# Cross-attention scores as three fp32r passes instead of one fp32 matmul, with a new order of work

## The chip, the cores and the metric

The kernel runs on one core of a Trainium2 chip. The metric is the device time of one execution in microseconds (us); TensorE (PE) multiplies matrices, and its weight loads (PEld) are a queue of their own in the profile; VectorE (DVE), ScalarE (ACT) and GpSimd (POOL) work on rows of 128 partitions; SyncE (SP) issues DMAs. TensorE writes only to PSUM, of which this kernel uses eight banks of 512 fp32 columns.

## The reference

One decoder layer on 32 batches of 112 tokens with 256 features, with a context of 375 rows per batch:

```python
x = x + attn(layernorm(x), W_qkv, W_out)                 # 16 heads of 16, window of 64, causal
x = x + xattn(layernorm(x), ctx, Wq, Wkv, Wo, rel_bias)  # 16 heads of 16
x = x + ffn(layernorm(x), router, gate, up, down)        # 8 experts, top 2

# xattn:
q = (h @ Wq).reshape(B, S, H, D).transpose(0, 2, 1, 3)
k, v = split((ctx @ Wkv).reshape(B, K, 2, H, D))
scores = einsum('bhsd,bhkd->bhsk', q, k) + bias
out = einsum('bhsk,bhkd->bshd', softmax(scores), v) @ Wo
```

The change touches `scores` of `xattn` alone: for each batch 16 heads, each 112x16 times 16x375.

## The kernel before

The program has two stages. Stage one runs both attentions and the router for the 32 batches and scatters the rows to expert buffers. Stage two (from L1050 on) runs 64 blocks of 128 rows through the experts.

Stage one is a software pipeline written out by hand. `PERIOD` lists the steps of one period, each with the batch it works on: `S0@1` in period i works on batch i+1. `plan` unrolls the list, and every engine runs those steps of the list that are its own, in this order. Nothing else sets the order: engines meet only at semaphores, so an `@` tells the order within an engine and not the time at which two engines run a step. A period is one batch of every step.

TensorE's steps, with the line that its matmuls carry: `xT`, `x2T`, `x3T`, `on`, `onC` (two transposes, L512); `qk` (L526); `v`, `wo`, `woc`, `rt` (L518); `S4`, the self scores (L535); `sT0` to `sT3` (four transposes, L544); `pvS` (L553); `ot`, `otc` (L560); `q2`, the cross queries (L568); `k0`, `k1`, the cross keys (L575); `v0`, `v1`, the context values (L583); `S0` to `S3`, the cross scores of four heads each (L594); `p0` to `p15` (three transposes of a head's scores, L603); `pv0` to `pv3` (L616); `pf` (L624, L625). In one period of before they stand in this order:

```
pv1 S0@1 p8 x3T@-1 p10 qk@3 sT0@2 p14 rt@-1 S1@1 sT3@2 sT1@2 k0@2 p15 pvS@2 p12 pv2 p13 p3@1 ot@2 pv3 p1@1 p0@1
on@2 pf@-1 S2@1 p7@1 wo@2 p2@1 k1@2 v0@2 otc p4@1 S3@1 onC p6@1 p5@1 x2T@2 woc v1@2 S4@3 pv0@1 q2@2 p11@1 v@3
xT@4 p9@1 sT2@3
```

PSUM banks: the four banks `S0` to `S3` are filled together by one group, `S0`..`S3` or `S4`, and hold one head (or four self heads) each. They are single: the next group waits until DVE has drained all four. Banks P and Q take turns for `sT` and `p`. Banks A and B take turns for all other TensorE steps (`BANK_AB`), so a bank must be drained two such steps later.

`cross_scores` (L588 to L596) makes one matmul for each of the four row tiles of 32 partitions: the stationary side is `q2`, 32x112 (the queries times a 0/-1 mask of half a row tile, two masks, made by ACT in `halves`, step `q2m`), the moving side is `k2`, 32x376, copied from the bank by ACT in steps `k0c`, `k1c`. Both are fp32. The trace shows an fp32 matmul as two LDWEIGHTS and two MATMUL rows.

`keys` and `context_values` already work in another way: context and weights are split into a high part, rounded to fp32r, and a low part, the remainder rounded to fp32r, and `PASSES` lists the three products that are added up: high by high, low by high, high by low. Each product is one LDWEIGHTS and one MATMUL row.

Behind the scores: DVE adds the bias and takes the minimum (steps `t0` to `t15`, L847), POOL subtracts (`u`, L466), TensorE transposes (`p`), ACT takes the exponential (`e`, L729), TensorE multiplies with the values (`pv`). DVE's other steps are `sm` (self scores, L835), the statistics `ln1` to `ln3`, the normalisations `nrm`, `nrmc` (L823, L824), the sums `x1` (L925) and `x2` (L947), `cl` (low part of the context, L936) and the router (`lg`, `rcA`, `rcB`, and `pfD` with L878 to L886).

Of the kernel before, what the change touches and what calls it, by code (L numbers as in the profile page):

```python
# [25 lines left out]
P = 128  # L26
# [37 lines left out]


PERIOD = """
t9@-1 e7@-1 pv1 xn@2 x1 su2@2 xn2 su0@2 v0c e2@-1 ln2 t11@-1 u10 e4@-1 t10@-1 nrmc@-2 oncc@-2 t12@-1 t15@-1
t14@-1 t13@-1 S0@1 x2Tc p8 su3@2 Lc@1 x2@-2 v1c ln3@-2 u1@1 e5@-1 ch@1 x3T@-1 e6@-1 oc0@-1 su1@2 q2m sm2@1
e11@-1 p10 sm0@1 sm3@1 qk@3 vc@1 e9@-1 xTc@2 sT0@2 p14 x3@-2 rt@-1 sm1@1 S1@1 t1 sT3@2 t3 sT1@2 k0@2 sE2@1 p15
pvS@2 p12 oc1@-1 e8@-1 t0 x3Tc@-2 pv2 t2 u0@1 e10@-1 p13 sE0@1 u3@1 p3@1 e14@-1 qkc@2 sE3@1 re@-2 cl@1 sE1@1  # L70
lg@-2 ot@2 pv3 p1@1 sc@-2 p0@1 e15@-1 on@2 pf@-1 S2@1 rcA@-2 p7@1 wo@2 p2@1 k1@2 ln1@3 u4@1 v0@2 otc u7@1
rs1@4 km@3 p4@1 u2@1 S3@1 u6@1 u5@1 onC u8@1 p6@1 k0c@1 t4 t7 p5@1 oTc@1 x2T@2 Lx@3 rs2@2 e12@-1 woc t5 u11@1
v1@2 u9@1 oc2@-1 S4@3 t6 pv0@1 nrm@1 u15@1 q2@2 e13@-1 e3 oc3@-1 p11@1 u14@1 e1 u13@1 rcB@-2 onc@1 st@-3 v@3
e0 xT@4 k1c@1 rs3 p9@1 pfD@-2 u12@1 sT2@3 t8
"""


# [33 lines left out]
def decoder_layer(nc, a, out):  # L111
# [21 lines left out]
    with ExitStack() as outer:  # L133
# [46 lines left out]
        with ExitStack() as st:  # L180
            def s1(name, shape, dt=F32):
                return sb(name, shape, dt, st)
# [46 lines left out]
            x1 = [sa([S, D]) for i in range(NX)]  # L229
            xn2 = sa([S, D])  # L230
            x2T = sa([P, DC, S])
            q2 = [sa([P, DC, 2, S]) for i in range(2)]

            cT = [s1(f"cT_{part}", [P, DC, TPAD], F32R) for part in ("high", "low")]
            wkv = [s1(f"wkv_{part}", [P, DC, 2 * D], F32R) for part in ("high", "low")]
            PASSES = ((0, 0), (1, 0), (0, 1))
            k2 = [sa([P, DC, T + 1]) for i in range(2)]
            v2 = [sa([TP, TC, H, HP]) for i in range(2)]
            z = [sa([S, TPAD]) for i in range(NZ)]
            mC = s1("mC", [S, H])  # L240
# [72 lines left out]
            s_sc = [sem("rows_scattered0"), sem("rows_scattered1")]  # L313
            s_padi = sem("padding_rows_known")

            NCONST, NLATE = 10, 9

            steps = [(w, b) for w, b in plan(B)]
            place = fills(steps)
            taken = {w: n for n, w in enumerate(w for w in steps if w[0][0] == "t" or w[0][:2] == "sm")}  # L320
            su_count = {w: n for n, w in enumerate(w for w in steps if w[0][:2] == "su")}
            u_count = {w: n for n, w in enumerate(w for w in steps if w[0][0] == "u")}

            had = {}
# [23 lines left out]
            def drain_sem(step, b):  # L348
                return drained[place[step, b][0]]
# [6 lines left out]
            def v3(t, n, w, m=P):  # L356

                return t[0:m, 0:n * w].rearrange("p (n w) -> p n w", n=n)

            with nc.Block() as block:  # L360
# [141 lines left out]
                def _(pe):  # L502
# [85 lines left out]
                    def cross_scores(g, b, F_):  # L588
                        if g == 0:
                            drained_wait(pe, "q2", b)  # L590
                        drained_wait(pe, f"k{g // 2}", b)
                        c, k = g // 2, g % 2
                        for r in range(HG):
                            m = pe.matmul(bank[f"S{r}"][0:S, 0:T + 1], q2[b % 2][32 * r:32 * r + 32, c, k, :],  # L594
                                          k2[b % 2][32 * r:32 * r + 32, c, :], start=True, stop=True)
                        m.then_inc(F_, 1)  # L596

                    def probs_back(n, b, B_, F_):
# [100 lines left out]
                def _(act):  # L699
# [14 lines left out]
                    def halves(b):  # L714
                        B_ = filled_wait(act, "q2", b)
                        if b >= 2:
                            filled_wait(act, "S3", b - 2)
                        for p in range(2):
                            m = act.activation(q2[b % 2][:, :, p, :], v3(B_, DC, S), ACT.Copy, scale=hmask[:, p:p + 1])
                        m.then_inc(drain_sem("q2", b), 1)  # L720

                    def cross_probs(n, b):
                        B_ = filled_wait(act, f"p{n}", b)
# [7 lines left out]
                    for step, b in steps:  # L731
# [5 lines left out]
                        elif step == "xTc":  # L737
                            drain("xT", b, xT[:, :, :], lambda t: v3(t, DC, S))
                        elif step == "qkc":
                            drain("qk", b, qk[:, :, :], lambda t: v3(t, 4, S))  # L740
                        elif step == "vc":
                            if b == 0:
                                need(act, s_pool, 1)
                            drain("v", b, vS[:, :, 0:DH], lambda t: v3(t, H, DH, S))
                        elif step[:2] == "sE":
                            r = int(step[2])
                            B_ = filled_wait(act, f"sT{r}", b)
                            if b:
                                filled_wait(act, "pvS", b - 1)
                            act.activation(pTF[r][:, :, :], v3(B_, HG, S, S), ACT.Exp, scale=SCALE)\  # L750
                               .then_inc(drain_sem(f"sT{r}", b), 1)
                        elif step == "oTc":
                            drain("pvS", b, oTF[:, :, :], lambda t: v3(t, NG, S))
                        elif step == "onc":
                            drain("on", b, onT[:, :, :], lambda t: v3(t, DC, S))
                        elif step == "xn2":
                            if b:
                                filled_wait(act, "x2T", b - 1)
                            normalised(1, b, x1[b % NX][:, :], [xn2[:, :]]).then_inc(s_xn2, 1)
                        elif step == "x2Tc":  # L760
                            drain("x2T", b, x2T[:, :, :], lambda t: v3(t, DC, S))
                        elif step == "q2m":
                            halves(b)
                        elif step == "ch":
                            need(act, s_c[b % 2], 16 * (b // 2 + 1))
                            if b:
                                for w in ("k0", "k1", "v0", "v1"):
                                    filled_wait(act, w, b - 1)
                            copy(cT[0][:, :, :], cin[b % 2][:, :, :], s_ch)
                        elif step in ("k0c", "k1c"):  # L770
                            if b >= 2:
                                filled_wait(act, "S3", b - 2)
                            drain(step[:2], b, k2[b % 2][:, int(step[1]), :], lambda t: t[:, 0:T + 1])
                        elif step in ("v0c", "v1c"):
                            if b >= 2:
                                filled_wait(act, "pv3", b - 2)
                            elif b == 0:
                                need(act, s_pool, 2)
                            if step == "v0c":
                                drain("v0", b, v2[b % 2][:, 0:2, :, 0:DH],  # L780
                                      lambda t: t[0:TP, 0:2 * D].rearrange("p (t h d) -> p t h d", t=2, h=H))
                            else:
                                drain("v1", b, v2[b % 2][:, 2, :, 0:DH], lambda t: v3(t, H, DH, TP))
                        elif step[:2] == "oc":
                            g = int(step[2])
                            if g == 0 and b:
                                filled_wait(act, "otc", b - 1)
                            drain(f"pv{g}", b, oTC[:, g, :], lambda t: t[:, 0:S])
                        elif step == "oncc":
                            drain("onC", b, otT[:, :, :], lambda t: v3(t, DC, S))  # L790
                        elif step == "x3":
                            if b >= 2:
                                need(act, s_sc[b % 2], 32 * (b // 2))
                            normalised(2, b, x2[b % 2][:, :], [x3[b % 2][k][:, 0:D] for k in (1, 0)]).then_inc(s_x3, 1)
                        elif step == "x3Tc":
                            drain("x3T", b, x3T[:, :, :], lambda t: v3(t, DC, S))
                        elif step == "re":
                            need(act, s_lg, b + 1)
                            B_ = filled_wait(act, "rt", b)
                            act.activation(ex[:, :], B_[0:S, 0:E], ACT.Exp, bias=nmx[:, :],  # L800
                                           accum_out=zs[:, :]).then_inc(drain_sem("rt", b), 1)
                        elif step[0] == "e":
                            cross_probs(int(step[1:]), b)

                @block.vector
                def _(dve):
# [102 lines left out]
                    for step, b in steps:  # L909
# [22 lines left out]
                        elif step == "cl":  # L932
                            if b == 0:
                                split_weights()
                            need(dve, s_ch, b + 1)
                            dve.tensor_tensor(cT[1][:, :, :], cin[b % 2][:, :, :], cT[0][:, :, :].bitcast(F32),  # L936
                                              ALU.subtract).then_inc(s_cl, 1)
                        elif step == "nrmc":
                            if b:
                                filled_wait(dve, "onC", b - 1)  # L940
# [344 lines left out]
```

## Time and profile before

| | us |
|---|---|
| median of the runs | 1370.25 (1369.9 to 1375.36) |
| profiled execution, its own time | 1372.08 |
| its span, first to last instruction | 1370.1 |
| TensorE busy in the span | 1269.7 (93%) |
| VectorE, ScalarE, GpSimd busy | 832.1, 717.7, 858.0 |
| mean granted TensorE clock | 0.966 |

Busy time is the union of an engine's instructions. Matmuls are pipelined, so a row of TensorE lasts longer than the time until the next may start; what a step costs on TensorE is read from its start to the start of the next step.

### The profile page before, as it was taken

The numbers are of one execution on the slowest core, as the hardware profiler recorded it, in microseconds if no ns is written. First come the engines' busy times: TensorE is split into PE (matmuls) and PEld (weight loads), VectorE is DVE, ScalarE is ACT, GpSimd is POOL, SyncE is SP. The second block draws the span as 40 slices with busy tenths as digits, with TensorE's granted clock in tenths as the row PEclk, the third lists the DMA queues.
The fourth block names the chain that finished last, engine by engine and source line by source line (L and its number), as shares of the span: only waits on it lengthen the run. The fifth ranks groups of instructions, "written<-read, shape, count | busy, mean of one in ns | idle before, by whom it ended". The sixth has DMA issues, their size and how long they took to land. (4 is left out here: it accounts for less than half of the span.)

```text
span 1370.1 us, 38959 instructions
## 1 busy us (share of the span) xinstructions
PE 1269.7 (93%) x13316; PEld 1069.7 (78%) x13317; DVE 832.1 (61%) x3821; ACT 717.7 (52%) x1827; POOL 858.0 (63%) x1597
## 2 busy tenths in 40 slices
PE   5499999999999999999999999996199999999993
PEld 3378888888878878878878888874099999999993
DVE  2247767777677767777677767765444444444441
ACT  2255666566665666566656666564044444444441
POOL 4266787778777787778777787775424444444431
PEclk9799999999999999999999999998599999999997
DMA  8910011010111111110101111000367223222224
GB/s 164 172 49 23 30 28 44 27 33 26 42 30 30 30 31 41 30 30 27 43 28 31 30 35 33 13 15 25 115 189 192 47 48 51 47 46 46 46 44 122
DMA packets 47310, 73.12 MB, mean 53 GB/s; under 512 B 6832, under 2 KB 34032, under 8 KB 47088
## 3 DMA queue, kind: packets, MB, share of 16 engines
q1 hardware_dynamic: 31408, 45.74, 12.4%
q0 software_dynamic: 15744, 25.31, 9.5%
q8 instruction: 94, 1.54, 0.5%
q14 instruction: 64, 0.52, 0.1%
HBM read 46.90 MB, written 27.80 MB: 55 GB/s over the span
## 5 line engine op out<-in xcount | busy, mean ns | idle before, releaser
L466 POOL TENSOR_SCALAR arena<-arena,mC 112x375 f32<-112x375 f32 x512 | 298.8, 593 | 156.7 <-DVE mC L847 154.5
L847 DVE CUSTOM_DVE_ANT_0 arena<-bank_S,arena 112x375 f32<-112x375 f32 x512 | 253.7, 543 | 113.9 <-PE bank_S L594 86.5
L1078 POOL DMA_INDIRECT acc<-y,xb x64 | 119.8, 1872 | 207.7 <-DVE y L1222 187.8
L472 POOL TENSOR_SCALAR arena<-arena,mF 112x112 f32<-112x112 f32 x512 | 201.3, 411 | 7.7 <-DVE mF L835 7.7
L701 ACT ACTIVATE arena<-bank_B 128x224 f32<-128x224 f32 (+6 forms) x260 | 101.0, 388 | 112.2 <-PE bank_B L575 53.8
L701 ACT ACTIVATE arena<-bank_A 128x224 f32<-128x224 f32 (+3 forms) x252 | 98.6, 391 | 106.7 <-PE bank_A L575 54.2
L1209 DVE SCALAR_TENSOR_TENSOR hT<-bankU,gub,gate 128x128 f32<-128x128 f32 x256 | 72.1, 344 | 109.3 <-PE bankU L1118 107.6
L594 PE MATMUL bank_S<-arena 32*112 32x376 f32 x1024 | 116.0, 522 | 19.1 <-DVE mC L847 18.8
L729 ACT ACTIVATE pTC<-bank_Q 126x336 f32<-126x336 f32 x256 | 115.0, 449 | 34.3 <-PE bank_Q L603 19.9
L1118 PE MATMUL bankG<-xbT,gwb 128*128 128x128 f32 x1024 | 126.6, 277 | 1.0 <-ACT gwb L1165 1.0
L1118 PE MATMUL bankU<-xbT,uwb 128*128 128x128 f32 x1024 | 125.8, 276 | 0.0
L603 PE MATMUL bank_Q<-ident,arena 112*126 112x112 f32 x768 | 123.9, 270 | 0.0
L1118 PEld LDWEIGHTS bankG<-xbT,gwb 128*128 128x128 f32 x1024 | 121.1, 194 | 1.4 <-issue 1.3
L1129 PE MATMUL bankY<-arena,hT 128*128 x512 | 120.9, 379 | 0.0
L1118 PEld LDWEIGHTS bankU<-xbT,uwb 128*128 128x128 f32 x1024 | 120.5, 193 | 0.0
L835 DVE CUSTOM_DVE_ANT_0 arena<-bank_S,window 112x112 f32<-112x112 f32 x512 | 102.1, 269 | 29.6 <-PE bank_S L535 29.6
L1159 ACT ACTIVATE xbT<-bankX 128x256 f32<-128x256 f32 x64 | 24.5, 383 | 182.2 <-PE bankX L1106 182.2
L603 PE MATMUL bank_P<-ident,arena 112*126 112x112 f32 x768 | 119.1, 264 | 0.2 <-ACT pTC L729 0.2
L603 PEld LDWEIGHTS bank_Q<-ident,arena 112*126 112x126 f32 x768 | 81.2, 140 | 47.7 <-issue 45.1
L729 ACT ACTIVATE pTC<-bank_P 126x336 f32<-126x336 f32 x256 | 114.4, 447 | 0.2
L1129 PEld LDWEIGHTS bankY<-arena,hT 128*128 128x128 f32 x512 | 92.4, 190 | 10.0
L603 PEld LDWEIGHTS bank_P<-ident,arena 112*126 112x126 f32 x768 | 84.8, 141 | 13.8 <-issue 6.2
(196 smaller groups left out, 2716.1 us busy)
## 6 DMA issues: line engine op xcount, KB each, us to landing
arena<-in_l_ctxT SPq DMA_DIRECT2D x32, 378.0 KB
xb<-xs POOLq DMA_DIRECT2D x64, 129.0 KB, 3.4
arena<-in_L_ffn_gate_w SPq DMA_DIRECT2D x8, 512.0 KB
arena<-in_L_ffn_up_w SPq DMA_DIRECT2D x8, 512.0 KB
arena<-in_L_ffn_down_w SPq DMA_DIRECT2D x8, 512.0 KB
arena<-in_x SPq DMA_DIRECT2D x32, 112.0 KB, 2.0
acc<-arena SPq DMA_DIRECT2D x32, 112.0 KB, 1.9
out<-acc SPq DMA_DIRECT2D x4, 896.0 KB, 9.2
```

What stands on the lines that cost most here:

```text
L466: pool.tensor_scalar(z[n % NZ][:, 0:T], z[n % NZ][:, 0:T], -1.0, mC[:, n:n + 1], ALU.mult, ALU.add).then_inc(s_u, 1)
L472: m = pool.tensor_scalar(sF[r][:, j, :], sF[r][:, j, :], -1.0, mF[:, r, j:j + 1], ALU.mult, ALU.add)
L594: m = pe.matmul(bank[f"S{r}"][0:S, 0:T + 1], q2[b % 2][32 * r:32 * r + 32, c, k, :], k2[b % 2][32 * r:32 * r + 32, c, :], start=True, stop ...
L603: m = pe.transpose(B_[0:TP, t * S:(t + 1) * S], z[n % NZ][:, t * TP:(t + 1) * TP], ident[0:S, 0:S])
L701: act.activation(dst, src, ACT.Copy).then_inc(then, 1)
L729: act.activation(pTC[n % NZ][:, :, :], v3(B_, TC, S, TP), ACT.Exp).then_inc(drain_sem(f"p{n}", b), 1)
L835: m = dve.tensor_tensor_reduce(out=sF[r][:, j, :], in0=t[:, j, :], in1=window[:, :], scale=1.0, scalar=3.0e38, op0=ALU.add, op1=ALU.min, a ...
L847: dve.tensor_tensor_reduce(out=z[n % NZ][:, 0:T], in0=bank[f"S{r}"][0:S, 0:T], in1=nbias[:, n, :], scale=1.0, scalar=3.0e38, op0=ALU.add, ...
L1078: pool.indirect_dma_start(out=acc[:, :], out_offset=bass.IndirectOffsetOnAxis(ap=xb[x][:, D + 1:D + 2].bitcast(I32), axis=0), in_=y2[x % 2 ...
L1118: m = pe.matmul(bk[q][:, f * P:(f + 1) * P], w[:, c, f * P:(f + 1) * P], xbT[q][:, c, :], start=(c == 0), stop=(c == DC - 1))
L1129: m = pe.matmul(bankY[q][:, 0:D], hT[q][:, c, :], w[:, c, :], start=(c == 0), stop=(c == FC - 1))
L1209: m = dve.scalar_tensor_tensor(hT[q][:, c, :], bankU[q][:, c * P:(c + 1) * P], gub[:, 1, bass.ds(e, 1), c:c + 1].rearrange("p o c -> p (o ...
```

## The change

The cross queries and keys are kept as a high and a low part in fp32r, and `cross_scores` adds three products in each of the four row tiles, one pass over all four tiles after another. ACT writes the high parts (`q2m`, `k0c`, `k1c` as before, now into fp32r). DVE has three new steps, `q2l`, `k0l` and `k1l`, that read the same bank again, subtract the high part and write the low part; it is now they that release the bank. `PERIOD` is another list.

```diff
-            q2 = [sa([P, DC, 2, S]) for i in range(2)]
-            k2 = [sa([P, DC, T + 1]) for i in range(2)]
+            q2 = [[s1(f"q2_{part}{i}", [P, DC, 2, S], F32R) for part in ("high", "low")] for i in range(2)]
+            k2 = [[s1(f"k2_{part}{i}", [P, DC, T + 1], F32R) for part in ("high", "low")] for i in range(2)]
...
-                        for r in range(HG):
-                            m = pe.matmul(bank[f"S{r}"][0:S, 0:T + 1], q2[b % 2][32 * r:32 * r + 32, c, k, :],
-                                          k2[b % 2][32 * r:32 * r + 32, c, :], start=True, stop=True)
+                        for u, w in PASSES:
+                            for r in range(HG):
+                                m = pe.matmul(bank[f"S{r}"][0:S, 0:T + 1], q2[b % 2][u][32 * r:32 * r + 32, c, k, :],
+                                              k2[b % 2][w][32 * r:32 * r + 32, c, :],
+                                              start=(u, w) == PASSES[0], stop=(u, w) == PASSES[-1])
                         m.then_inc(F_, 1)
...
-                            m = act.activation(q2[b % 2][:, :, p, :], v3(B_, DC, S), ACT.Copy, scale=hmask[:, p:p + 1])
-                        m.then_inc(drain_sem("q2", b), 1)
+                            m = act.activation(q2[b % 2][0][:, :, p, :], v3(B_, DC, S), ACT.Copy, scale=hmask[:, p:p + 1])
+                        m.then_inc(s_qh, 1)
+
+                    def keys_high(o, b):
+                        B_ = filled_wait(act, f"k{o}", b)
+                        if b >= 2:
+                            filled_wait(act, "S3", b - 2)
+                        act.activation(k2[b % 2][0][:, o, :], B_[:, 0:T + 1], ACT.Copy).then_inc(s_kh, 1)
...
+                        elif step == "q2l":
+                            need(dve, s_qh, b + 1)
+                            for p in range(2):
+                                m = dve.scalar_tensor_tensor(q2[b % 2][1][:, :, p, :], v3(bank[place["q2", b][0]], DC, S), hmask[:, p:p + 1],
+                                                             q2[b % 2][0][:, :, p, :].bitcast(F32), ALU.mult, ALU.subtract)
+                            m.then_inc(drain_sem("q2", b), 1)
+                        elif step in ("k0l", "k1l"):
+                            o = int(step[1])
+                            need(dve, s_kh, kh_count[f"k{o}c", b] + 1)
+                            dve.tensor_tensor(k2[b % 2][1][:, o, :], bank[place[f"k{o}", b][0]][:, 0:T + 1],
+                                              k2[b % 2][0][:, o, :].bitcast(F32), ALU.subtract).then_inc(drain_sem(f"k{o}", b), 1)
```

The new list, cut to TensorE's steps and to DVE's:

```
TensorE: sT0@3 pv2@1 pv1@1 S0@2 pf@-1 p14@1 v0@2 sT1@3 p12@1 S1@2 pvS@3 v@4 p15@1 p13@1 ot@3 k1@3 p3@2 pv3@1 S2@2
x3T p2@2 on@3 p1@2 otc@1 p0@2 k0@3 wo@3 p7@2 p6@2 onC@1 S4@4 pv0@2 rt p4@2 woc@1 p9@2 p10@2 x2T@3 xT@5 p8@2 p5@2
q2@3 S3@2 qk@5 p11@2 sT2@4 v1@3 sT3@4
DVE: t15 q2l@1 t14 t12 ln1@4 t13 rcB@-2 t2@1 t1@1 t3@1 t0@1 pfD@-2 t4@1 cl@2 t6@1 t5@1 nrm@2 t7@1 k1l@2 t11@1
t10@1 nrmc t8@1 t9@1 k0l@2 x1@2 ln2@2 sm3@3 lg@-1 sm2@3 x2 sm1@3 sm0@3 ln3 rcA@-1
```

## Rows read from the trace of the kernel before

**Rows 1.** The page: the span, and busy time of each engine.
```profile
span 1370.1 us, 38959 instructions
PE 1269.7 (93%) x13316; PEld 1069.7 (78%) x13317; DVE 832.1 (61%) x3821; ACT 717.7 (52%) x1827; POOL 858.0 (63%) x1597
```
**Rows 2.** Busy time by stretch: PE, PEld, DVE, ACT, POOL, then clock, DMA share, GB/s.
```profile
502.90:530.90 28.00, 28.00 (x333) 22.55 (x332) 20.53 (x105) 17.16 (x45) 21.46 (x46) 1.00 0.12 33
...
934.00:962.00 28.00, 16.39 (x184) 11.58 (x181) 13.34 (x70) 10.24 (x29) 10.77 (x18) 0.78 0.09 26
...
985.00:1370.10 385.10, 357.12 (x2688) 339.69 (x2688) 166.08 (x448) 164.82 (x385) 157.77 (x128) 0.96 0.39 85
```
**Rows 3.** TensorE in order of time: start, length, what (sT2, pv1, S0, p8, x3T, p10, qk).
```profile
507.19 0.55 PE L544 MATMUL bank_P<-ident,arena 112*112 112x112 f32 x4
507.67 0.78 PE L616 MATMUL bank_B<-pTC,arena 126*32 126x112 f32 x24
508.38 0.90 PE L594 MATMUL bank_S<-arena 32*112 32x376 f32 x8
509.21 0.51 PE L603 MATMUL bank_Q<-ident,arena 112*126 112x112 f32 x3
509.56 0.35 PE L512 MATMUL bank_A<-ident,arena 112*128 112x112 f32 x2
509.75 0.45 PE L603 MATMUL bank_P<-ident,arena 112*126 112x112 f32 x3
510.04 1.95 PE L526 MATMUL bank_B<-arena 128*128 128x112 f32 x16
```
**Rows 4.** TensorE at 508.97: the second half of the same cross-score group.
```profile
508.79 0.49 PE L594 MATMUL bank_S<-arena 32*112 32x376 f32 x4
```
**Rows 5.** TensorE: the first three of six fp32r passes of the keys, k0.
```profile
514.48 0.42 PE L575 MATMUL bank_B<-cT_high,wkv_high 128*128 128x376 f32 x1
514.73 0.33 PE L575 MATMUL bank_B<-cT_low,wkv_high 128*128 128x376 f32 x1
514.90 0.33 PE L575 MATMUL bank_B<-cT_high,wkv_low 128*128 128x376 f32 x1
```
**Rows 6.** Self scores S4 at 503.37: matmuls of a set, and weight loads then running.
```profile
503.19 0.37 PE L535 MATMUL bank_S<-arena 32*112 32x224 f32 x4
503.20 0.18 PEld L535 LDWEIGHTS bank_S<-arena 32*112 32x112 f32 x3
```
**Rows 7.** The same at 503.56: the next set of four.
```profile
503.38 0.37 PE L535 MATMUL bank_S<-arena 32*112 32x224 f32 x4
```
**Rows 8.** TensorE around k1 and v0: p2, k1's first, v0's first three.
```profile
523.20 0.45 PE L603 MATMUL bank_P<-ident,arena 112*126 112x112 f32 x3
523.62 0.44 PE L575 MATMUL bank_B<-cT_high,wkv_high 128*128 128x376 f32 x1
...
524.89 0.38 PE L583 MATMUL bank_A<-wkv_high,cT_high 128*126 128x256 f32 x1
525.11 0.28 PE L583 MATMUL bank_A<-wkv_high,cT_low 128*126 128x256 f32 x1
525.22 0.28 PE L583 MATMUL bank_A<-wkv_low,cT_high 128*126 128x256 f32 x1
```
**Rows 9.** Waits of the weight loads from 200 to 850 us: total, times, longest.
```profile
PEld bank_B L583 <- DVE arena L925: 3.3, 12, 0.3
```
**Rows 10.** VectorE groups that read PSUM and SBUF: count, busy us, mean ns.
```profile
L847 DVE CUSTOM_DVE_ANT_0 arena<-bank_S,arena 112x375 f32<-112x375 f32 x512 | 253.7, 543 | 113.9 <-PE bank_S L594 86.5 <-DMA arena<-skew 19.0 <-PE bank_P L603 6.3
...
L1209 DVE SCALAR_TENSOR_TENSOR hT<-bankU,gub,gate 128x128 f32<-128x128 f32 x256 | 72.1, 344 | 109.3 <-PE bankU L1118 107.6 <-ACT gate L1173 1.5
```
**Rows 11.** VectorE in order of time: first and last operation of pfD.
```profile
521.27 0.17 DVE L878 TENSOR_TENSOR rank<-bank_B,run 112x8 f32<-112x8 f32 x1
...
523.40 0.16 DVE L886 TENSOR_TENSOR run<-bank_B,run 128x8 f32<-128x8 f32 x1
```
**Rows 12.** The start of stage one: what VectorE waits for.
```profile
65.52 0.55 DVE L847 CUSTOM_DVE_ANT_0 arena<-bank_S,arena 112x375 f32<-112x375 f32 x1 [19.02 <-DMA arena<-skew]
```

More of the change, by code:

```diff
@@ L66 @@
 PERIOD = """
[L67 to L74, printed above, removed]
+rs1@3 sT0@3 e15@-1 t15 u14@-1 pv2@1 u12@-1 q2l@1 t14 t12 ln1@4 e13@-1 x3@-2 k1c@1 u13@-1 st@-2 t13 rcB@-2 t2@1
+t1@1 t3@1 e3 oc3@-1 xn@3 km@2 u1 u3 t0@1 x3Tc@-2 u2 Lc@2 rs3@-2 e2 pfD@-2 onc@1 pv1@1 e1 t4@1 e0 S0@2 cl@2
+k0c@1 t6@1 e7 t5@1 nrm@2 oncc@-1 e6 t7@1 k1l@2 pf@-1 u0 oc0 u6 u4 u7 u5 sc@-3 e4 p14@1 re@-2 xn2@1 u8 v0@2 e9
+e10 x2Tc@1 Lx@5 sT1@3 p12@1 e8 S1@2 pvS@3 u9 xTc@3 u10 u11 e5 v@4 rs2@1 p15@1 q2m@1 p13@1 qkc@3 e11 ot@3 t11@1
+t10@1 k1@3 sE2@2 nrmc p3@2 t8@1 pv3@1 t9@1 v1c@1 S2@2 k0l@2 sE3@2 x1@2 x3T p2@2 su3@2 ln2@2 oc2 on@3 sm3@3
+p1@2 otc@1 lg@-1 sE0@2 su2@2 p0@2 oc1 sm2@3 k0@3 x2 sm1@3 sm0@3 wo@3 p7@2 p6@2 su0@2 u15 ln3 onC@1 S4@4 pv0@2
+rcA@-1 e14 v0c@1 sE1@2 rt p4@2 woc@1 p9@2 p10@2 ch@2 x2T@3 xT@5 p8@2 p5@2 e12 oTc@2 q2@3 S3@2 qk@5 p11@2 sT2@4
+v1@3 vc@3 sT3@4 su1@2
 """
@@ L314, in decoder_layer @@
             s_padi = sem("padding_rows_known")
+            s_qh = sem("cross_queries_high_ready")
+            s_kh = sem("cross_keys_high_ready")
             NCONST, NLATE = 10, 9
@@ L321, in decoder_layer @@
             su_count = {w: n for n, w in enumerate(w for w in steps if w[0][:2] == "su")}
+            kh_count = {w: n for n, w in enumerate(w for w in steps if w[0] in ("k0c", "k1c"))}
             u_count = {w: n for n, w in enumerate(w for w in steps if w[0][0] == "u")}
@@ L770, in _ @@
                         elif step in ("k0c", "k1c"):
-                            if b >= 2:
-                                filled_wait(act, "S3", b - 2)
-                            drain(step[:2], b, k2[b % 2][:, int(step[1]), :], lambda t: t[:, 0:T + 1])
+                            keys_high(int(step[1]), b)
                         elif step in ("v0c", "v1c"):
```

## The prediction

> **What bounds the kernel now.** I read the page first: TensorE is busy for 93% of the span, every other engine for 63% or less [rows 1]. A share can mix stages, so the second view was busy time by stretch. In the middle of stage one a period is 28.00 us, and TensorE is busy for all of it at a clock of 1.00, VectorE for 20.53 us, POOL for 21.46 us [rows 2]. The steps repeat with a period of 27.99 us. The third view, TensorE in order of time, shows that nearly all of this is work and not waiting. So stage one's middle is bounded by TensorE's sum of steps. Its start is bounded by something else: VectorE waits 19 us for the bias DMA and goes on at 65.5 us [rows 12]. Its end (934 us on) is a chain through all engines with TensorE busy for 16.39 of 28 us [rows 2]. Stage two, 385 us, is not touched by the change [rows 2].
>
> A step costs its start to the next start. The cross-score group S0 costs 509.21-508.38 = 0.83 us [rows 3]. Its second half starts at 508.79 [rows 4], so the halves take 0.41 and 0.42 us. A half streams 376 fp32 columns in two cycles each: 752 cycles at 2.4 GHz, 0.313 us. The four row tiles run beside each other: four matmuls of the half go out as one packet, and 4x0.313 would be 1.25 us. What is left, 0.83-0.63 = 0.20 us, is the first weight load, which nothing covers, and the drain before the next step in another tile mode.
>
> **The passes.** Three passes replace two halves. The nearest rows for a pass of 376 fp32r columns are those of k0: 514.90-514.73 = 0.17 us, against 0.157 us of streaming [rows 5]. They are of 128 rows and not of four tiles of 32. So the new group costs 3x0.171+0.204 = 0.717 us, 0.115 us less than 0.832. Bounds: 0.157 a pass gives 0.675; a pass held to the pace of the self scores' sets, 503.38-503.19 = 0.19 us [rows 6, 7], gives 0.77. With four groups in a period I take 4x0.115 = 0.46 us (between 0.25 and 0.63).
>
> Weights are loaded twelve times a group and no longer eight. Whether a load hides is decided by the rows of S4, which has the same shape of weights: the loads for the next set start at 503.20, right behind the running set's start at 503.19, in the same row tiles, and the next set starts 0.19 us after the running one, where its 224 columns stream for 0.187 us [rows 6, 7]. They are hidden, so I add nothing. The Trainium skill speaks against this: "TensorE: Matmul & The Clock Gate", section "Part 3: Packing small matmuls", says that a weight load overlaps a running matmul only if the row group differs. The trace of the self scores disagrees. By the rule the load of 112 columns would stand before each pass, and that is a rival below.
>
> **The new order on TensorE.** The steps are the same 48, so only their borders change. Three kinds of border have a price in the trace.
> - Entering a tiled step (S, S4, pv, pvS) from an untiled one: sT2 before pv1 costs 507.67-507.19 = 0.48 us [rows 3], where four transposes are 0.38 (x3T's two take 0.19). So 0.095 us each. The old order enters 8 times, the new one 6: -0.19 us.
> - Leaving one: p8 after S0 costs 0.35 us, p10 after x3T 0.29 us [rows 3], so 0.055 us in front of transposes, and some 0.09 in front of matmuls, which is what the exposed first load of S0 costs (0.41-0.313) [rows 3, 4]. Old order seven and one, new order some four and three: -0.10 us.
> - Two tiled steps of one mode in a row, pv2 and pv1 in the new order: no drain (0.42-0.313 = 0.11 at S0 [rows 3, 4]) and no slow first set (some 0.03) between them: -0.14 us.
>
> Together -0.43 us. The old order also holds small waits. p2 in front of k1 costs 0.42 us for 0.29; k1, six passes that would be 1.03, costs 524.89-523.62 = 1.27; v0's first pass 0.22 for the 0.12 of its next one [rows 8]: 0.47 us, partly since v0's load waits for the sum x1 on VectorE to release the bank [rows 9]. These are properties of the old order, and in the new one k0, k1, v0 and v1 each have a transpose or a projection in front. I count -0.47+0.05 = -0.42 us for them, and what the new order waits for is counted next.
>
> **VectorE and the banks.** New work: `k0l`, `k1l` of 128x376 and `q2l` of twice 128x224. An operation on 375 columns from PSUM and SBUF takes 543 ns, and a scalar_tensor_tensor on 128 columns, also from both, 344 ns [rows 10]; so 0.55 us for a key half and, at 0.8 to 1 ns a column more, 0.42 to 0.44 us for a half of q2l. As back-to-back starts are some 90 ns closer than lengths, that is 0.5+0.5+0.8 = 1.8 us a period. VectorE goes from 20.5 to 22.4 us of about 27: not the bound, but its queue is fuller, and three banks now go free only after ACT and then VectorE. I laid the new order out without waits, a step behind the other, and looked at where the next user of a bank comes:
> - k0's bank goes to onC behind wo, p7 and p6. From k0's start that is 1.04+0.87+0.29+0.29 = 2.5 us (six passes, four fp32 matmuls of 256 columns, twice three transposes). The bank is free after k0's last end (1.26), ACT's copy (0.5), k0l (0.55), and VectorE is at t9 until then: 2.4 to 2.5 us. A wait of about 0.1.
> - q2's bank goes to v1 and x2's to xT: about 0.1 each.
> - pf's bank goes to pvS, behind p14, v0, sT1, p12 and S1: 3.6 us after pf starts. pfD stands behind t2, t1, t3, t0 on VectorE and took 523.56-521.27 = 2.3 us [rows 11]; its 0.17 us operations with nothing beside them would make 1.3. From pf's start the four t of S0's banks are done at about 2.0 (0.47 each), so pfD is at 3.3 to 4.3: a wait between 0 and 0.6; I take 0.15, nearer to the quiet case since the planned neighbours on POOL aren't known. Queued behind this wait on TensorE are pvS and all that follows.
> - k1's bank (to x3T) and the S banks between S4 and S3 (sixteen self scores, x2 and lg on VectorE) have 0.2 to 0.4 us to spare.
> That is +0.45 us, 0 to 1.0. The new steps have no cover to lose elsewhere: ACT does the same copies, POOL and the queues of SP have the same steps.
>
> **Sum.** 27.99-0.46-0.43-0.42+0.45 = 27.13 us, 0.86 less. The middle lasts from about 67 us to 924 us, 30.5 periods: 26.2 us. Start: the bias still lands at 65.5 us, and the new order has about 0.8 us more of TensorE's work in front of S1 of batch 0: -0.8. End: the last batch's chain has the same steps; nothing. Stage two: nothing. The profiled execution took 1372.1 us (span 1370.1 and 2 us around it) and would take 1345; it lies 1.8 us above the median of the runs, so the forecast is 1370.25-27 = 1343 us.
>
> The Trainium skill would make more of the passes. "FP8 and Floating Point Precision", section "TensorE Precision Notes", has true fp32 as four passes, and "TensorE: Matmul & The Clock Gate", "Back-to-back issue gap", has N/2.4+2.5 ns for one. By both an estimate of the group is 3x0.159+0.204 = 0.68 us, and the sum would be some 4.5 us lower; the fp32r rows of k0 stand 12 ns above that rule for each pass, and they decide.
>
> **Rivals.**
> - New waits eat what the order gives (chance 0.18). For it: VectorE and POOL would both be above 80% busy, the S banks are single, and four turnarounds have less than 0.2 us to spare. Against: the old order shows hardly any waits at 73% and 77%. Only the passes' gain is left, 30.5x0.46 = 14 us: 1356 us (1350 to 1363).
> - Weight loads are not hidden in a tile that runs (0.05). Mechanism: each pass costs its streaming and a load like the exposed one of S0, 0.171+0.094. The group is 0.717+0.188 = 0.905 us, slower than now; 4x0.188x30.5 = 23 us on top of 1343: 1366 us. It is the rule of the Trainium skill weighed above.
> - Slower: fp32r passes of different row tiles don't run beside each other (0.08). No row here has fp32r in row tiles; all tiled rows are fp32. The place is each of the 128 groups: twelve matmuls of 0.171 and 0.20 are 2.26 us for 0.72, 1.54x128 = 197 us: 1540 us. It decides from a pass of 0.24 us: with the 0.4 us that borders and waits give back, a group may cost 0.93 us, (0.93-0.20)/3 = 0.24. Against it: fp32 matmuls of the four tiles do overlap, and each tile has a bank of its own.
> - The change does what it says but waits grow to the old period (0.07): within 6.9 us of 1370.
>
> **How the numbers follow.** Forecast (0.62): 1343 us, itself between 1330 (no new waits, 0.157 a pass) and 1352. Half a per cent, 6.9 us, is about what a measurement of this kernel can tell from no change. Faster by more: 0.62+0.18 and a part of the others, 0.82. Within: 0.08. Slower: 0.10, the third rival and waits beyond the old period. The range holds the forecast and the first rival: 1328 to 1363.
>
> **What would show it.** Middle periods of about 27.1 us, TensorE busy throughout; L594 with twelve matmul rows in a group, passes 0.17 us apart and 0.72 us to the next step; k0l, k1l near 550 ns; waits of TensorE's loads on L594's neighbours no longer than 0.3 us; the first t0 still at 65 us; stage two at 385 us. Passes farther apart than 0.19 us, a period above 27.6 us, or a wait on VectorE in front of pvS or onC longer than 0.3 us would make the forecast wrong, each at the term that it belongs to.

## The result and the profile after

| | before | after |
|---|---|---|
| median of the runs, us | 1372.75 (4 runs) | 1334.44 (1333.07 to 1335.83, 4 runs) |
| ratio to before | 1 | 0.9721, interval 0.9692 to 0.975 |
| span of the profiled execution, us | 1370.1 | 1331.8 |
| middle period, us | 27.99 | 26.95 |

The change is worth 38 us; 27 were forecast. One more run of before than was known ahead moved its median from 1370.25 to 1372.75 us. After lies in the range given (1328 to 1363). The experiments were run in three rounds, each with its own runs of before (median 1372.39 us for the order alone, the passes alone, the order of the twelve matmuls and the count update; 1369.58 us for the four that follow; 1373.36 us for the last two). Times of different rounds are therefore compared to some 3 us, and the periods in the traces are the finer measure.

The span of after, the busy time of its engines, and one middle period (columns as in rows 2); they answer to [rows 1, 2]:

```profile
span 1331.8 us, 40106 instructions
...
PE 1227.9 (92%) x13828; PEld 1090.0 (82%) x13829; DVE 870.9 (65%) x3949; ACT 728.9 (55%) x1827; POOL 859.0 (65%) x1597
```
```profile
466.43:493.38 26.95, 26.71 (x352) 23.24 (x348) 21.70 (x108) 17.51 (x46) 21.53 (x46) 1.00 0.12 33
```

TensorE is still the bound of the middle, now with 0.24 us of idle time in a period. VectorE does 21.70 us of work in 26.95 instead of 20.53 in 28.

TensorE of after in order of time, through the cross-score group S1 and into pvS and v; this answers to [rows 3, 4]. LDWEIGHTS rows of a group (S2, at 476.11) stand below it:

```profile
470.09 0.43 PE L599 MATMUL bank_S<-k_high,q_high 32*112 32x376 f32 x4
470.35 0.34 PE L599 MATMUL bank_S<-k_high,q_low 32*112 32x376 f32 x4
470.53 0.33 PE L599 MATMUL bank_S<-k_low,q_high 32*112 32x376 f32 x4
471.10 0.97 PE L557 MATMUL bank_B<-arena 112*32 112x112 f32 x32 [0.24 <-DVE run L896]
```
```profile
476.11 0.18 PEld L599 LDWEIGHTS bank_S<-k_high,q_high 32*112 32x112 f32 x4 [0.17 <-issue]
476.20 0.18 PEld L599 LDWEIGHTS bank_S<-k_high,q_low 32*112 32x112 f32 x4
476.38 0.18 PEld L599 LDWEIGHTS bank_S<-k_low,q_high 32*112 32x112 f32 x4
```

Each group is three sets of four tiles. The second set starts 0.26 us after the first, an interval that holds the exposed load, and the third 0.17 to 0.18 us after the second, which is the cost of a pass. Group S2 starts at 476.11 and the next step at 476.81: 0.70 us for the old 0.83. The weights of the third pass are loaded from 476.38 on, while the second pass runs from 476.37 in the same four tiles, and the third starts 0.17 us later. In S1 the next step, pvS, starts 1.01 us after the group and not 0.70: it waits 0.31 us (0.30 on the mean of the middle periods) for VectorE's update of the running counts, which releases pf's bank.

Where the 38.3 us of the span went, by the starts of S0 of a batch (a batch's `pf` is its last TensorE step of stage one):

| stretch | before | after | difference |
|---|---|---|---|
| to S0 of batch 1 | 89.86 | 91.17 | +1.3 |
| S0 of batch 1 to S0 of batch 31 | 834.09 | 800.17 | -33.9 |
| to the last pf | 37.87 | 33.41 | -4.5 |
| from there to the end | 408.28 | 407.05 | -1.2 |

### The profile page after: what moved, and what is told of

Read it like the earlier page. It is cut to its first block and busy times, and to the rows that moved or that the text cites. A ratio compares the mean times of both kernels' runs of the same rounds, so it can differ in the third digit from the quotient of the medians.

```text
span 1331.8 us, 40106 instructions
## 1 busy us (share of the span) xinstructions
PE 1227.9 (92%) x13828; PEld 1090.0 (82%) x13829; DVE 870.9 (65%) x3949; ACT 728.9 (55%) x1827; POOL 859.0 (65%) x1597
## 5 line engine op out<-in xcount | busy, mean ns | idle before, releaser
L857 DVE CUSTOM_DVE_ANT_0 arena<-bank_S,arena 112x375 f32<-112x375 f32 x512 | 264.9, 543 | 112.6 <-PE bank_S L599 64.8
L476 POOL TENSOR_SCALAR arena<-arena,mF 112x112 f32<-112x112 f32 x512 | 177.6, 367 | 22.8 <-DVE mF L845 21.2
L741 ACT ACTIVATE pTC<-bank_Q 126x336 f32<-126x336 f32 x286 | 128.6, 450 | 45.7 <-PE bank_Q L609 44.5
L707 ACT ACTIVATE arena<-bank_B 128x224 f32<-128x224 f32 (+5 forms) x229 | 87.4, 382 | 110.0 <-PE bank_B L530 35.0
L707 ACT ACTIVATE arena<-bank_A 128x224 f32<-128x224 f32 (+3 forms) x219 | 82.2, 376 | 112.0 <-PE bank_A L622 28.1
L609 PE MATMUL bank_Q<-ident,arena 112*126 112x112 f32 x858 | 130.8, 261 | 0.5 <-ACT pTC L741 0.5
L741 ACT ACTIVATE pTC<-bank_P 126x336 f32<-126x336 f32 x226 | 102.0, 451 | 37.9 <-PE bank_P L609 37.6
L609 PE MATMUL bank_P<-ident,arena 112*126 112x112 f32 x678 | 104.4, 262 | 0.8 <-ACT pTC L741 0.8
L609 PEld LDWEIGHTS bank_Q<-ident,arena 112*126 112x126 f32 x858 | 97.9, 143 | 6.9 <-issue 1.5
L1186 ACT ACTIVATE gwb<-arena 128x1024 f32 x64 | 67.8, 1060 | 29.1 <-issue 28.7
```

The costliest lines, as they stand in the source:

```text
L476: m = pool.tensor_scalar(sF[r][:, j, :], sF[r][:, j, :], -1.0, mF[:, r, j:j + 1], ALU.mult, ALU.add)
L609: m = pe.transpose(B_[0:TP, t * S:(t + 1) * S], z[n % NZ][:, t * TP:(t + 1) * TP], ident[0:S, 0:S])
L707: act.activation(dst, src, ACT.Copy).then_inc(then, 1)
L741: act.activation(pTC[n % NZ][:, :, :], v3(B_, TC, S, TP), ACT.Exp).then_inc(drain_sem(f"p{n}", b), 1)
L857: dve.tensor_tensor_reduce(out=z[n % NZ][:, 0:T], in0=bank[f"S{r}"][0:S, 0:T], in1=nbias[:, n, :], scale=1.0, scalar=3.0e38, op0=ALU.add, ...
L1186: act.activation(gwb[q][:, :], package(e, "gw"), ACT.Copy).then_inc(s_gw, 1)
```

## The experiments

Theory A, with the prediction: in the middle of stage one the time is TensorE's sum of steps and borders, so whatever shortens a group or removes a border is won in full, and what holds a bank longer costs only where the next user would have come earlier. The rivals differ from run to run.

### The order alone

Edit: the kernel before with the new `PERIOD` without `q2l`, `k0l`, `k1l`; the cross scores are the fp32 matmul.

```diff
- PERIOD of before
+ PERIOD of after, without q2l@1, k1l@2 and k0l@2
```

> The new order without its three low-part steps, and the cross scores as one fp32 matmul again. Theory A (passes and order each have a share, and the middle is TensorE's sum of steps): a group costs 0.83 us again for 0.70, so a middle period is 26.95 + 4x0.13 = 27.5 us, and the time is that of the changed kernel, 1334.4, plus 30.5x0.53 = 16 us: 1351 us, 22 us below the kernel before. Rival B (the order is only there to make room for the low parts): the period is the old 27.99 us and the time within 5 us of the kernel before.

Measured: 1341.44 us, ratio 0.9784 (0.9761 to 0.9808), a middle period of 27.17 us. That is 31 us below before: B is out, and more than A had it. A added to the period of the changed kernel, which holds the wait in front of pvS, and here there is no such wait. The rows show it at S1 (TensorE in order of time): the fp32 group takes its 0.84 us, and pvS follows at once.

```profile
473.69 0.90 PE L594 MATMUL bank_S<-arena 32*112 32x376 f32 x8
474.53 0.59 PE L553 MATMUL bank_B<-arena 112*32 112x112 f32 x16
```

The wait of 0.31 us in front of pvS appears only when the passes and their low parts come in. So the order gives 27.99-27.17 = 0.82 us a period, the passes 4x0.13 = 0.52, and the new wait takes 0.30 back. What VectorE does behind pf shows where the wait comes from: the first and the last operation of `pfD`, with the order alone (pf starts at 470.74) and in after (pf starts at 467.13):

```profile
472.76 0.16 DVE L878 TENSOR_TENSOR rank<-bank_B,run 112x8 f32<-112x8 f32 x1
...
474.30 0.16 DVE L886 TENSOR_TENSOR run<-bank_B,run 128x8 f32<-128x8 f32 x1
```
```profile
469.13 0.16 DVE L888 TENSOR_TENSOR rank<-bank_B,run 112x8 f32<-112x8 f32 x1
...
470.89 0.16 DVE L896 TENSOR_TENSOR run<-bank_B,run 128x8 f32<-128x8 f32 x1
```

VectorE takes up `pfD` 2.0 us after pf in both. So the low parts don't hold it up in the queue there. With the order alone `pfD` is done 3.72 us after pf and pvS starts at 3.79, 0.07 us behind; in after, where pvS waits for it, it starts 0.05 us behind, so the order alone had only some 0.02 us to spare. In after `pfD` lasts 1.92 us instead of 1.70, and S1 is 0.13 us shorter, so that pvS is ready sooner. These two make up the wait. Why `pfD` lasts longer isn't shown. By these rows the shorter group would bring a wait of some 0.1 us without any low parts, an estimate that wasn't tried.

The end shrinks with the order alone too: from S0 of batch 31 to the last pf 33.81 us, against 37.87 before and 33.41 after.

### The passes alone

Edit: the changed kernel with the old order, each low part put where VectorE can do it first.

```diff
- ... sm0@1 sm3@1 qk@3 ... rcA@-2 p7@1 ... ln1@3 ... ln2 t11@-1 ...
+ ... sm0@1 sm3@1 q2l qk@3 ... rcA@-2 p7@1 ... k0l@1 ln1@3 ... ln2 k1l t11@-1 ...
```

> The three passes in the old order, with the low-part steps put on VectorE as soon as their high parts are written. Theory A (a bank that two engines drain one after another comes free too late in the old order): q2's bank is wanted by xT 0.2 us after the high part is written and the low part takes 0.8 us, and k0's bank by pv2 while VectorE chooses the experts; I expect waits of about 0.8 and 0.5 us a period against 0.53 us that the passes give, so a period of 28.5 to 28.8 us and a time 15 to 25 us above the kernel before. Rival B (the passes pay by themselves): a period of about 27.5 us, a time 16 us below the kernel before.

Measured: 1399.59 us, ratio 1.0201 (1.0175 to 1.0226), a middle period of 28.98 us: 27 us slower than before. B is out; A has the kind of effect right, but its 15 to 25 us were too few. The group is 0.70 us here as well, so the passes do give their 0.52 us; the waits take 1.5 us. TensorE in order of time shows the largest, xT behind v, which comes 1.6 us after v where v costs 0.87; then TensorE's waits from 300 to 800 us (total, times, longest):

```profile
522.85 1.03 PE L522 MATMUL bank_B<-arena 128*112 128x256 f32 x4
524.45 0.41 PE L516 MATMUL bank_A<-ident,arena 112*128 112x112 f32 x2 [0.57 <-DVE q_low L951]
```
```profile
PE bank_B L516 <- DVE q_low L951: 5.1, 9, 0.6
PE bank_A L516 <- DVE q_low L951: 4.5, 8, 0.6
PE bank_B L579 <- DVE run L896: 2.8, 9, 0.3
...
PE bank_A L622 <- DVE k_low L957: 1.6, 9, 0.2
```

Two of the three places are those that were expected: the waits of xT and pv2 cost some 0.7 and 0.25 us a period, for the 0.8 and 0.5 of A. The third is k1 behind pf's release, with 0.35 us more than in before. Here too VectorE takes up `pfD` as soon after pf as in before (0.53 us), `pfD` lasts 0.22 us longer, and S2 in front of k1 is 0.13 us shorter. The places of q_low and k_low were chosen with care but not searched for, so this bounds what the old order can do with the passes only from one side.

### The order of the twelve matmuls

```diff
-                        for u, w in PASSES:
-                            for r in range(HG):
+                        for r in range(HG):
+                            for u, w in PASSES:
```

> The same twelve matmuls of a cross-score group, but all three passes of one row tile before the next tile. Theory A (matmuls run beside each other only when neighbours in the queue are in different row tiles): the last pass of one tile and the first of the next overlap, nine pass times are left of twelve, 9x0.17+0.2 = 1.7 us a group for 0.70, four groups x 30.5 x 1.0 = 125 us more: 1460 us. Rival B (TensorE starts what is ready whatever stands in front of it): no change from 1334 us. Rival C (no overlap at all): 12x0.17+0.2 = 2.25 us a group, 1523 us.

Measured: 1334.38 us (one run), B. The program has tile 0's three passes, then tile 1's; the trace has this (TensorE, then its weight loads, of group S2):

```profile
475.70 0.45 PE L599 MATMUL bank_S<-k_high,q_high 32*112 32x376 f32 x4
475.96 0.35 PE L599 MATMUL bank_S<-k_high,q_low 32*112 32x376 f32 x4
476.13 0.35 PE L599 MATMUL bank_S<-k_low,q_high 32*112 32x376 f32 x4
```
```profile
475.96 0.20 PEld L599 LDWEIGHTS bank_S<-k_low,q_high 32*112 32x112 f32 x4
```

The first matmuls of all four tiles start first, 10 ns apart where it was 3, then the four second ones, then the third. By the trace a matmul of tile 1 passes the second and third of tile 0 that stand before it in the program. That this order is made on the chip and not when the program is built isn't shown by itself; the wider spacing of the first four speaks for the chip. The change isn't quite free: group S2 costs 0.72 us here for 0.70. The period is the same 26.95 us, in part because pvS waits 0.04 us less.

### The count update moved forward

```diff
                         link(dve.tensor_tensor(rank[:, :], B_[0:S, 0:E], run[0:S, :], ALU.add))
+                        dve.tensor_tensor(run[:, :], B_[:, E:2 * E], run[:, :], ALU.add).then_inc(drain_sem("pf", b), 1)
...
-                        dve.tensor_tensor(run[:, :], B_[:, E:2 * E], run[:, :], ALU.add).then_inc(drain_sem("pf", b), 1)
```

> The update of the running counts, which releases pf's bank, moved from the end of pfD to right behind its first operation. Theory A (the 0.31 us that pvS waits in each period is for this release and nothing stands close behind it): a period of 26.65 us, 30.5x0.3 = 9 us less, 1325 us. Rival B (something else, the exponentials for pvS or the S banks, comes 0.1 us later): the wait changes its name and 3 us or less are won.

Measured: 1325.52 us, ratio 0.9662 (0.9637 to 0.9687), a middle period of 26.66 us. A, to the microsecond. The same place in TensorE's order, and the busy time from 300 to 800 us of this kernel:

```profile
465.71 0.35 PE L599 MATMUL bank_S<-k_low,q_high 32*112 32x376 f32 x4
465.99 0.97 PE L557 MATMUL bank_B<-arena 112*32 112x112 f32 x32
```
```profile
300.00:800.00 500.00, 500.00 (x6550) 435.47 (x6549) 404.77 (x2016) 328.59 (x845) 404.52 (x844) 1.00 0.12 33
```

TensorE is busy for all of the 500 us, and VectorE and POOL for 81%. Busy time doesn't mean that no wait is left: in front of x2T some 0.1 us remain, see the last experiment. Of the kernels that compute all three products this is the fastest, 9 us faster than the change and 47 us faster than before. Of the six runs that follow, the first adds the same edit to the order alone, and the others build on this kernel.

> The new order with the fp32 cross scores and without low parts, and the early update of the counts. Theory A (pvS waits for the counts only where VectorE has the low parts to write as well): nothing to gain, a period of 27.17 us, 1341.4 us; the three passes are then worth 1341.4-1325.5 = 16 us once this wait is out of the way. Rival B (the order itself carries this wait): some 9 us less, 1332 us.

Measured: 1342.24 us, a period of 27.16 us, so nothing (1341.44 us without the edit). B is out: the order itself has no such wait. A's number is right, but this kernel lacks the low parts and also has the longer fp32 group, so it doesn't show that the low parts alone make the wait. With the wait out of the way the passes are worth 1342.2-1325.5 = 17 us (0.51 us a period), and with the wait in place 1341.4-1334.4 = 7 us.

### Two passes, four passes

On the kernel with the count update moved forward. The diff is that of two passes; for four, SCORES is `((0, 0), (1, 0), (0, 1), (1, 1))`, with the low part of both operands in the last.

```diff
+            SCORES = ((0, 0), (1, 0))
...
-                        for u, w in PASSES:
+                        for u, w in SCORES:
...
-                                              start=(u, w) == PASSES[0], stop=(u, w) == PASSES[-1])
+                                              start=(u, w) == SCORES[0], stop=(u, w) == SCORES[-1])
```

> The kernel with the early update of the counts, and in the cross scores only the first two products: high by high and low queries by high keys. The product with the low keys is left out of the computation; the low keys are still written. Theory A (a pass costs 0.17 us of TensorE in each group and TensorE is still the bound): a period of 26.66-4x0.17 = 25.98 us, 30.5x0.68 = 21 us less than 1325.5: 1305 us. Rival B (VectorE and the single S banks are next, close behind): the period stays above 26.3 us, 1316 us or more, with waits of the cross scores for VectorE.

> The same kernel with a fourth product, low by low. Theory A (0.17 us a pass): a group of 0.87 us, a period of 27.34 us, 1325.5+21 = 1346 us; the group is then slower than the fp32 matmul's 0.83. Rival B (the chip's fp32 matmul is no dearer than four fp32r passes, since it streams four times as well): the group is 0.83 us and the time 1341.5.

Measured: 1307.51 us with a period of 26.06, and 1348.36 us with a period of 27.34: A in both. TensorE at group S2, with two and with four passes; the next step is the last row of each:

```profile
462.64 0.43 PE L600 MATMUL bank_S<-k_high,q_high 32*112 32x376 f32 x4
462.90 0.34 PE L600 MATMUL bank_S<-k_high,q_low 32*112 32x376 f32 x4
463.18 0.32 PE L517 MATMUL bank_A<-ident,arena 112*128 112x112 f32 x1
```
```profile
481.26 0.43 PE L600 MATMUL bank_S<-k_high,q_high 32*112 32x376 f32 x4
481.52 0.34 PE L600 MATMUL bank_S<-k_high,q_low 32*112 32x376 f32 x4
481.69 0.34 PE L600 MATMUL bank_S<-k_low,q_high 32*112 32x376 f32 x4
481.86 0.34 PE L600 MATMUL bank_S<-k_low,q_low 32*112 32x376 f32 x4
482.13 0.41 PE L517 MATMUL bank_A<-ident,arena 112*128 112x112 f32 x2
```

Groups of 0.54, 0.70 and 0.87 us: a pass is 0.17 us, and the border 0.19 us. Upwards a pass costs 1348.4-1325.5 = 23 us (the period says 0.68x30.5 = 21), downwards it gives 18 us for the 21 expected. At two passes the period is 0.08 us longer than the sum, so something else begins to be late there. In the trace the step behind S1 comes 0.61 us after it for 0.53; what it waits for isn't shown. Four fp32r passes (0.87) are dearer than one fp32 matmul (0.83) of this shape.

### The low part twice

```diff
-                            dve.tensor_tensor(k2[b % 2][1][:, o, :], bank[place[f"k{o}", b][0]][:, 0:T + 1],
-                                              k2[b % 2][0][:, o, :].bitcast(F32), ALU.subtract).then_inc(drain_sem(f"k{o}", b), 1)
+                            low = lambda: dve.tensor_tensor(k2[b % 2][1][:, o, :], bank[place[f"k{o}", b][0]][:, 0:T + 1],
+                                                            k2[b % 2][0][:, o, :].bitcast(F32), ALU.subtract)
+                            if o == 0:
+                                link(low())
+                            low().then_inc(drain_sem(f"k{o}", b), 1)
```

> The same kernel, with the low part of the first key half written twice, 0.55 us more on VectorE and the second write 0.06 us behind the first. Theory A (k0's bank is free only 0.17 us before onC wants it): onC waits 0.4 us in each period, 30.5x0.4 = 12 us more: 1337 us. Rival B (VectorE has 5 us of idle time a period, so half a microsecond is hidden): no change from 1325.5 us.

Measured: 1341.24 us, a period of 27.18 us: 15.7 us more, so A, with 0.52 us a period for the 0.4 expected. In the changed kernel the low part of k0 and the next user of its bank, onC, stand so (VectorE, then TensorE with its weight load), and below them onC with the low part written twice:

```profile
480.32 0.55 DVE L957 TENSOR_TENSOR k_low<-bank_B,k_high 128x376 fp32r<-128x376 f32 x1 [0.21 <-ACT k_high L732]
```
```profile
480.95 0.24 PEld L516 LDWEIGHTS bank_B<-ident,arena 112*128 112x128 f32 x2
481.04 0.35 PE L516 MATMUL bank_B<-ident,arena 112*128 112x112 f32 x2
```
```profile
484.24 0.41 PE L516 MATMUL bank_B<-ident,arena 112*128 112x112 f32 x2 [0.30 <-DVE k_low L957]
```

The bank is free at 480.87 and onC's matmul starts at 481.04. But its weight load, which waits for the bank too (this run shows it 0.51 us idle for k_low), starts at 480.95 already, and in this run it starts 0.06 us behind the release. So the changed kernel had 0.02 us to spare here and not the 0.17 of the expectation, and that is why the whole second write shows. VectorE has 5 us of idle time in a period, and half a microsecond at this place costs half a microsecond all the same.

### Borders

```diff
- rs1@3 sT0@3 e15@-1 t15 u14@-1 pv2@1 u12@-1
+ rs1@3 pv2@1 e15@-1 t15 u14@-1 sT0@3 u12@-1
```

> The kernel with the early update of the counts, and sT0 moved from in front of the pair pv2, pv1 to between the two; nothing else. Theory A (each border between a tiled and an untiled step has a price): pv2 now drains before sT0 (+0.11), sT0's first load is exposed (+0.05), pv1 is entered anew (+0.12), so the period is 26.66+0.28 = 26.94 us and the time 1325.5+8.5 = 1334 us. Rival B (borders cost nothing that other work doesn't hide; the new order is better for its fewer waits alone): no change from 1325.5 us.

Measured: 1334.85 us, ratio 0.9718 (0.9702 to 0.9735), a period of 26.94 us: 9.3 us and 0.28 us a period more, A (8.5 us by the period). TensorE of this kernel (sT3, pv2, sT0, pv1, S0):

```profile
490.99 0.55 PE L548 MATMUL bank_Q<-ident,arena 112*112 112x112 f32 x4
491.47 0.78 PE L622 MATMUL bank_A<-pTC,arena 126*32 126x112 f32 x24
492.18 0.59 PE L548 MATMUL bank_P<-ident,arena 112*112 112x112 f32 x4
492.71 0.78 PE L622 MATMUL bank_B<-pTC,arena 126*32 126x112 f32 x24
493.42 0.44 PE L599 MATMUL bank_S<-k_high,q_high 32*112 32x376 f32 x4
```

pv2 costs 0.71 us where it was 0.60 in front of pv1, and sT0 between two tiled steps 0.53 us where it was 0.48 in front of pv2 alone. sT3, now in front of pv2, costs 0.48 us for 0.38.

### An attempt at the last wait

```diff
- e4 p14@1 re@-2 xn2@1 u8
+ xn2@1 e4 p14@1 re@-2 u8
```

> The kernel with the early update of the counts, and ACT's step xn2 two places earlier, in front of e4 and re. Theory A (the 0.12 us that x2T loses in each period are for xn2, which stands behind re on ACT): 30.5x0.1 = 3 us less, 1322.5 us. Rival B (re, which drains the bank that x2T takes, becomes the later one, or e4 delays p9): no change, or up to 3 us more.

Measured: 1327.86 us, ratio 0.9669 (0.9654 to 0.9684), beside 0.9662 for the kernel that it builds on; the period is the same 26.66 us. B: p10 in front of x2T costs 0.28 us for 0.37, so the wait was indeed for xn2. But xT, p8 and p5 behind it cost 0.23, 0.34 and 0.34 us for 0.19, 0.29 and 0.31, and lose what x2T wins; for what they wait isn't shown:

```profile
481.57 0.35 PE L516 MATMUL bank_A<-ident,arena 112*128 112x112 f32 x2
481.80 0.51 PE L609 MATMUL bank_Q<-ident,arena 112*126 112x112 f32 x3
482.14 0.51 PE L609 MATMUL bank_P<-ident,arena 112*126 112x112 f32 x3
482.48 0.61 PE L572 MATMUL bank_B<-arena 128*128 128x112 f32 x4
```

## Why the prediction was right, and where it was short

- **What bounds the kernel: right.** Between the kernels in the new order the time moves by 30.5 times what TensorE's period moves, within 2.5 us (four passes: 0.68 us a period, so 21 us, for 23 measured). Between those in the old order, 0.99 us a period would be 30 us, and 27 were measured (the two profiled spans differ by 29.8). Between the two orders there are 6 us more, those of the end, below.
- **The passes: right, one term too large.** A pass was put at 0.171 us and is 0.17. The border was put at 0.204 us, the fp32 group's, and is 0.19. The group costs 0.70 us for the 0.717 forecast: 0.52 us a period for 0.46.
- **No other mechanism in the group: right.** fp32r passes of the four tiles run beside each other, and the loads into running tiles are hidden. The rule of the Trainium skill that spoke against it ("TensorE: Matmul & The Clock Gate", "Part 3: Packing small matmuls") doesn't hold here: the loads at 476.38 and the matmuls at 476.37 are in the same row groups, and the next pass is not late.
- **The order: right in sum, by terms that were off both ways.** Forecast were 0.43 us of borders and 0.42 of old waits, together 0.85, and the order alone gives 0.82. Step by step it is made up otherwise, and the next three points say how.
- **Borders: the prices right, the counts wrong.** The step "the new one 6" entries miscounted: the new order enters tiled steps at pv2, S1, pv3, S4 and S3, five times, as S2 stands right behind pv3. That is 0.095 us more. It leaves them five times too, once in front of transposes (x3T) and four times in front of matmuls (pf, v, rt, qk). The forecast's "four and three" would by its own prices cost 0.02 us more than the old order and not 0.10 less; five exits, counted rightly, give 0.06 less. With the next two points some 0.54 us of what the order gives are left for the borders, for 0.43. The prices were tried by themselves: 0.28 us forecast and 0.28 measured for the split pair.
- **Old waits: partly not waits.** Of the 0.47 us at p2, k1 and v0 some 0.3 are gone (p2 0.42 to 0.29, k1 1.27 to 1.12, v0 1.51 to 1.50). The rest is what these steps cost in either order: k1 was held against 1.03 us, but k0 of before, which has the same six passes, already takes 515.60-514.48 = 1.12 us, and v0's first pass takes 0.20 us in after too (467.82 to 468.02). On the other side onC, p6 and p5 of before held 0.1 us that was left out, and it is gone.
- **New waits: the sum right, the places not.** Forecast 0.45 us: onC 0.1, xT and v1 0.1 each, pvS 0.15 of 0 to 0.6. Measured are two: pvS with 0.30, and 0.12 in front of x2T (p10 0.38 for 0.29, x2T 0.22 for 0.19, as the last experiment tells), which the order alone has too. onC, xT and v1 wait for nothing. The wait at pvS is as long as the one that was named as a sign against the forecast ("longer than 0.3 us").
- **The period.** It came out at 26.95 us for 27.13. 0.06 us of this are the passes, 0.03 the other way the order, and 0.15 are that the passes with their low parts brought one wait of 0.30 us in place of 0.45 in four places. The forecast's lower end of 1330 us is worked out wrongly as well: without new waits and with 0.157 us a pass, its own terms give 1324.
- **Low parts on VectorE: right.** 550 and 445 ns for 550 and 420 to 440, as these rows of VectorE's groups in after show. k0's bank was thought to be free 2.4 to 2.5 us after k0's start, for a use at 2.5; it is free at 2.39, its next weight load starts at 2.47 and the matmul at 2.56.

```profile
L957 DVE TENSOR_TENSOR k_low<-bank_B,k_high 128x376 fp32r<-128x376 f32 x33 | 18.1, 550 | 9.9 <-ACT k_high L732 9.9
...
L951 DVE SCALAR_TENSOR_TENSOR q_low<-bank_A,hmask,q_high 128x224 fp32r<-128x224 f32 x38 | 15.3, 445 | 1.8 <-ACT q_high L725 1.8
```

- **Start: open.** The bias still lands late (VectorE goes on at 65.59 us for 65.52). Forecast were 0.8 us less; S0 of batch 1 starts 1.3 us later, but 63 TensorE steps stand in front of it for 58, so the two starts don't mark the same amount of work. No run separates the two.
- **End: wrong.** "The last batch's chain has the same steps; nothing" left out 4.5 us behind S0 of batch 31, and the last two periods before it shrank by 4.1 us, twice as much as two middle periods. The steps are the same, but not what stands between them. Busy time from S0 of batch 31 to the last pf, before and after:

```profile
923.95:961.82 37.87, 24.61 (x293) 17.12 (x289) 20.55 (x108) 16.27 (x47) 17.41 (x28) 0.84 0.08 25
```
```profile
891.34:924.75 33.41, 23.66 (x290) 18.42 (x291) 22.58 (x124) 15.68 (x44) 19.34 (x33) 0.89 0.10 29
```

TensorE's busy time is 0.95 us less of these 4.5; the rest is idle time that went. The order alone has it too (33.81 us), so it belongs to the order. From the first matmul of the last pf but one to that of the last pf it is 961.82-947.70 = 14.1 us before and 924.75-918.96 = 5.8 us after. Between the two the old order has otc, onC, woc, x3T and rt of the last batch, the new one only x3T and rt. That this closes the gap wasn't tried.

Of the 11 us by which the forecast fell short, 5.5 are the period (0.18 us in 30.5 periods), some 6 to 7 the end with its last two periods, and the start (2.1 us the other way) and stage two (1.2 us) nearly cancel out.

## What to carry to other kernels

Where one engine is busy nearly without a gap, its sum of start-to-start costs predicted this change to a hundredth of the period, though the borders between kinds of steps were miscounted and part of what was taken for waiting was cost. In the order's share those errors nearly cancelled, which is luck. So the borders have to be priced and counted as well as the steps, and a wait is a wait only against the same step elsewhere in the trace. The ends of the pipeline need a sum of their own: 6 of the 38 us came from there, and the forecast had nothing for them. An edit that makes work cheaper on that engine by adding a little work to another one must be looked at where a buffer is released: the same three passes are worth 27 us less than nothing in one order, 7 us in another, and 17 us once one release is moved ahead of five small operations. Average idle time of the other engine (here a fifth) says nothing on that.

## What the runs showed of the hardware that was not expected

- By this trace TensorE does not keep the order of matmuls in different row tiles. With three passes of one tile standing in the program before the first of the next, the four first ones still started 10 ns apart (at 475.70) and the time was the same, 1334.4 us in one run. The Trainium skill, "TensorE: Matmul & The Clock Gate", "Part 3: Packing small matmuls", has matmuls in strict order of the program; this trace disagrees.
- An fp32r pass of 376 columns takes 0.17 us in four row tiles of 32 as in one of 128, 0.014 us above its 376 columns at 2.4 GHz. So four of them are 5% dearer than one fp32 matmul of the same shape (groups of 0.87 and 0.83 us).
